# Adding the exponentials of two key tiles on GpSimd, with one set of products with ones for two tiles, in a four-layer graph network on one Trainium2 core

## The reference

```python
def _L1_gnn_ref(h, adj, Wq, bq, Wk, bk, Wv, bv, Wo, bo):
    ...
    scores = jnp.einsum('bhqd,bhkd->bhqk', q, k) * scale
    scores = jnp.where(mask, -jnp.inf, scores)
    attn = jax.nn.softmax(scores, axis=-1)
    out = jnp.einsum('bhqk,bhkd->bhqd', attn, v)
    ...
```

## Time and profile before

| | |
|---|---|
| median of 3 runs | 3092.38 us (3091.72 to 3095.64) |
| the profiled execution | 3093.04 us, its span 3091.3 us |
| TensorE busy | 2725.8 us, 88% of the span |
| VectorE busy | 2070.4 us, 67% |
| ScalarE busy | 1223.4 us, 40% |
| GpSimd busy | 824.4 us, 27% |
| mean granted TensorE clock | 0.943 |
| one step in the middle of the run | 181 us |

### The profile page before, as it was taken

How to read it: one execution, slowest core, us unless ns; L and a number is a source line. 1 busy time by engine, 2 the same in 40 slices (tenths; PEclk the granted TensorE clock), 3 DMA queues, 4 the chain that set the end, 5 groups by cost and what they waited for, 6 DMA issues and landing times.

```text
span 3091.3 us, 47649 instructions
## 1 busy us (share of the span) xinstructions
PE 2725.8 (88%) x17668; PEld 2029.7 (66%) x17668; DVE 2070.4 (67%) x5503; ACT 1223.4 (40%) x2273; POOL 824.4 (27%) x640
## 2 busy tenths in 40 slices
PE   0679989899998989989898998989899998989976
PEld 0447776767767676766767677676767767676664
DVE  3547485775848677584867758486775858677563
ACT  0224435353443535344352543435254343524341
POOL 0113231322313232232323222232322323232231
PEclk9889989999898999989899998989999898999987
DMA  4000000000000000000000000000000000000000
GB/s 124 7 14 1 8 14 1 15 8 15 8 8 14 1 15 8 15 8 8 14 1 15 8 15 8 8 14 1 14 8 15 8 8 14 1 8 8 1 8 7
DMA packets 29763, 36.74 MB, mean 12 GB/s; under 512 B 2272, under 2 KB 23648, under 8 KB 29536
## 3 DMA queue, kind: packets, MB, share of 16 engines
q1 hardware_dynamic: 29536, 33.69, 3.7%
HBM read 25.30 MB, written 8.39 MB: 11 GB/s over the span
## 4 chain that ended last, share of the span: by engine, by line
PE 57%; DVE 23%; issue 8%; ACT 6%; POOL 4%; SPq 1%; DMA 1%; DVEq 0%; POOLq 0%; ACTq 0%
PE bank L587 12%; PE bank L546 9%; PE bank L784 7%; DVE bank L1077 5%; PE bank L673 4%; PE bank L561 4%; PE bank L679 4%; PE bank L540 4%; PE bank L663 3%; PE bank L656 3%; POOL exp_b L472 3%; DVE picked L1044 2%; PE bank L793 2%; DVE o_t L1121 2%; PE bank L713 2%
## 5 line engine op out<-in xcount | busy, mean ns | idle before, releaser
L472 POOL TENSOR_TENSOR exp_b<-exp_b,edge_t 128x512 int32<-128x512 int32 x320 | 455.0, 1437 | 1075.9 <-DVE exp_b L1065 1075.9
L587 PE MATMUL bank<-vals_b,exp_b 128*128 128x257 f32 x2560 | 662.6, 404 | 75.4 <-POOL exp_b L472 67.3
L587 PEld LDWEIGHTS bank<-vals_b,exp_b 128*128 128x128 f32 x2560 | 483.4, 198 | 231.8 <-POOL exp_b L472 117.7
L923 ACT ACTIVATE h_sb<-bank,rden_g_b 128x256 f32<-128x256 f32 x320 | 151.6, 474 | 692.5 <-DVE rden_g_b L1221 692.5
L1077 DVE CUSTOM_DVE_ANT_0 bank<-bank,edge_bias 128x512 f32<-128x512 f32 x512 | 338.9, 720 | 22.4 <-PE bank L605 21.5
L1065 DVE TENSOR_TENSOR exp_b<-exp_b,low_b 128x512 f32<-128x512 f32 x320 | 271.6, 870 | 93.1 <-ACT low_b L839 90.8
L1044 DVE CUSTOM_DVE_ANT_0 picked<-bank,edge_bias 128x512 bf16<-128x512 f32 x384 | 241.5, 683 | 108.9 <-PE bank L561 108.9
L871 ACT ACTIVATE exp_a<-bank 128x512 f32<-128x512 f32 x512 | 263.9, 608 | 89.4 <-PE bank L663 89.4
L818 ACT ACTIVATE vals_b<-bank 128x512 f32<-128x512 f32 (+1 forms) x192 | 100.9, 536 | 485.5 <-PE bank L784 280.7
L460 POOL TENSOR_TENSOR rstd_a<-var_eps_a,neg_half 128x4 f32<-128x4 f32 x48 | 51.2, 1067 | 777.5 <-DVE var_eps_a L1021 777.5
L784 PE MATMUL bank<-wo_sb,ht_all 128*128 128x259 f32 x1024 | 233.6, 383 | 0.8 <-ACT ht_all L818 0.8
(11 more groups left out here) (185 smaller groups left out, 5409.5 us busy)
## 6 DMA issues: line engine op xcount, KB each, us to landing
x_t<-in_x_t SPq DMA_DIRECT2D x16, 512.0 KB, 3.6
xa<-in_x SPq DMA_DIRECT2D x16, 512.0 KB, 3.7
out<-h_sb SPq DMA_DIRECT2D x16, 512.0 KB, 2.9
exp_b<-in_adj SPq DMA_DIRECT2D x1, 1024.0 KB, 7.1
edge_t<-in_adj_t SPq DMA_DIRECT2D x1, 1024.0 KB, 9.2
wo_sb<-in_L_gnn_W_out SPq DMA_DIRECT2D x1, 1024.0 KB, 11.7
ht_all<-in_L_gnn_a_heads SPq DMA_DIRECT2D x4, 256.0 KB, 8.6
exp_a<-in_L_gnn_W_heads SPq DMA_DIRECT2D x2, 512.0 KB, 4.3
```

The source lines that it names most:

```text
L472: pool.tensor_tensor(high_exp(idx, j).bitcast(I32), high_exp(idx, j).bitcast(I32), edge_t[:, j, :], ALU.mult)\
L587: last = pe.matmul(bank(key)[:, i * width:(i + 1) * width], high_exp(idx, c)[:, t * P:(t + 1) * P], vals[:, c, 0:width], start=c == 0, sto ...
```

## The change

GpSimd adds the exponentials of key tiles 0 and 1, and of 2 and 3, head by head, into a new tile `pair_sum` (four adds of 128x512 for each of two pairs and two groups: 16 in a batch). TensorE runs its products with ones only in `pv` g 1 and `pv` g 3, on `pair_sum`. There is one `pair_sum`, so GpSimd waits for the products on the old one (`summed`, or the product of `sum`). ScalarE, before it writes over a tile of `exp_a`, waits for the products with the values and for the add that read it. `TURNS` is a new string. The tiles `first_row` and `wa`, used in the setup alone, move into `exp_b` to make room.

```diff
-TURNS = ("b2 t m3 t b2 m b m b t m b t b m3 b6 m2 a3 b m2 a m2 b2 s b2 a b a m b s b a m s a s2 a2 m s2 b s b2 s a2 m b3 m3 b2 a "
...
+TURNS = ("b2 t m3 b t b m b m b m t b3 m3 b t b m b2 m b m2 a2 b a2 m2 b3 s b a b2 m a s b a m s a s a2 m s2 b s b2 s a2 b m b2 "
...
+        pair_sum = sb("pair_sum", [P, HG, N])
...
+                for g in range(G1):
+                    for t in range(1, T, 2):
+                        for p in parts["st"]:
+                            yield "st", g, t, p
+                            for hh in heads_of("st", p):
+                                pool.wait_ge(*after(b, moved(("st", g, t, hh))))
+
+                                if t == T - 1:
+                                    pool.wait_ge(*after(b, sig.value("summed", g)))
+                                else:
+                                    for count in earlier(b, product_of(("sum", (g - 1) % G1), 0 if g else -1)):
+                                        pool.wait_ge(*count)
+                                pool.tensor_tensor(pair_sum[:, hh, :], exp1(g, t - 1, hh), exp1(g, t, hh), ALU.add)\
+                                    .then_inc(sig.raised("pair_added", (g, t // 2, hh)), 1)
...
-                    for hh in range(HG):
-                        at = slice(hh * D1, (hh + 1) * D1)
-                        last = pe.matmul(bank(("sum", g))[at, :], ones[:], exp1(g, t, hh), start=t == 0, stop=t == T - 1)
...
+                    if t % 2:
+                        for hh in range(HG):
+                            at = slice(hh * D1, (hh + 1) * D1)
+                            pe.wait_ge(*after(b, sig.value("pair_added", (g, t // 2, hh))))
+                            last = pe.matmul(bank(("sum", g))[at, :], ones[:], pair_sum[:, hh, :], start=t == 1, stop=t == T - 1)
+                        last.then_inc(filled(("sum", g)) if t == T - 1 else sig.raised("summed", g), 1)
...
+                        if old >= 0:
+                            if hh == 0:
+                                act.wait_ge(*after(b, product_of(("o", old // T)) if old % T == T - 1 else sig.value("weighed", (old // T, old % T))))
+                            act.wait_ge(*after(b, sig.value("pair_added", (old // T, old % T // 2, hh))))
```

More of the change, by code:

```diff
@@ L22 @@
 STREAMS = {"p": "pre", "m": "mid", "s": "second", "b": "back", "a": "att", "t": "tail"}
-TURNS = ("b2 t m3 t b2 m b m b t m b t b m3 b6 m2 a3 b m2 a m2 b2 s b2 a b a m b s b a m s a s2 a2 m s2 b s b2 s a2 m b3 m3 b2 a "
-         "m a m s m b2 a b m a b m a m b m a2 m a3 m a m a m a p m2 a m2 a m a m b p m2 b2 m b2 m b p m a4 m p a m a p m a2 p2 a "
-         "p a")
+TURNS = ("b2 t m3 b t b m b m b m t b3 m3 b t b m b2 m b m2 a2 b a2 m2 b3 s b a b2 m a s b a m s a s a2 m s2 b s b2 s a2 b m b2 "
+         "s b m3 b a m2 a2 b s m b2 m a b m b m a m a2 m a m a3 m a m a2 m4 a m a m b p m2 p b2 m b m b2 p m a4 m a p a m a2 p2 "
+         "m a p a p")
 AHEAD = {"pre": 2, "mid": 1, "second": 1, "back": 0, "att": 0, "tail": -1}
@@ L103, in gat_mix_program @@
         ident_r = sb("ident_r", [P, P], F32R)
-        first_row = sb("first_row", [P, P])
         first_row_r = sb("first_row_r", [P, P], F32R)
@@ L176, in gat_mix_program @@
         ah_bc = ht_all[:].rearrange("p a n -> p (a n)")[:, 0:H3 * 2 * F].rearrange("p (h j f) -> p h j f", j=2, f=F)
+        A_END = 2 * H0 + 2 * F
+        first_row = a_bc[:, A_END:A_END + P]
+        wa = a_bc[:, A_END + P:A_END + P + KF * 3 * H3].rearrange("p (k c) -> p k c", k=KF)
         adj_i = exp_b[:, SLOTS - T:SLOTS, :].bitcast(I32)
@@ L674, in weigh @@
                                          start=t == 0, stop=t == T - 1)
-                    if t == T - 1:
-                        last.then_inc(filled(("o", g)), 1)
-                    for hh in range(HG):
-                        at = slice(hh * D1, (hh + 1) * D1)
-                        last = pe.matmul(bank(("sum", g))[at, :], ones[:], exp1(g, t, hh), start=t == 0, stop=t == T - 1)
-                    if t < T - 1:
-                        last.then_inc(sig.raised("weighed", (g, t)), 1)
-                    else:
-                        last.then_inc(filled(("sum", g)), 1)
+                    last.then_inc(filled(("o", g)) if t == T - 1 else sig.raised("weighed", (g, t)), 1)
+                    if t % 2:
[4 more added lines that the diff above has]
+                        last.then_inc(filled(("sum", g)) if t == T - 1 else sig.raised("summed", g), 1)
                 yield "q", 0
@@ L866, in exps1 @@
                     for hh in heads_of("st", p):
-                        key, at = ("st", g, t, hh), g * T + t - 2
-                        for count in highest(b, product_of(key), *([] if hh else [sig.value("weighed", (at // T,
-                                             at % T)) if at >= 0 and at % T < T - 1 else product_of(("sum", at // T)) if at >= 0 else product_of("a01")])):
-                            act.wait_ge(*count)
+                        key, old = ("st", g, t, hh), g * T + t - 2
+                        act.wait_ge(*after(b, product_of(key)))
+                        if old >= 0:
+                            if hh == 0:
+                                act.wait_ge(*after(b, product_of(("o", old // T)) if old % T == T - 1 else sig.value("weighed", (old // T, old % T))))
+                            act.wait_ge(*after(b, sig.value("pair_added", (old // T, old % T // 2, hh))))
+                        elif hh == 0:
+                            act.wait_ge(*after(b, product_of("a01")))
                         act.activation(exp1(g, t, hh), bank(key)[:], ACT.Exp, scale=SCALE1).then_inc(emptied(key), 1)
@@ L1288, in program @@
     def program(order):
-        nc = _bacc.Bacc("TRN2", target_bir_lowering=False, num_devices=1, dynamic_dma_scratch_size=4096)
+        nc = _bacc.Bacc("TRN2", target_bir_lowering=False, num_devices=1, dynamic_dma_scratch_size=2048)
         arrays, args = {}, []
```

1 line of the change is left out of this document (removed).

## The result

The changed kernel takes 3255.91 us (median of 4 runs, 3246.62 to 3260.62), beside 3092.55 us for the kernel before (3091.72 to 3095.64): 1.0523 times as long, interval 1.0498 to 1.0547. It is 163 us slower. The prediction said slower by 55 us, with a range up to 3205, so the direction was right and the size was not.

A forecast was written before the change was run, and what follows sets the result against it. TensorE was taken as the bound in mid-step, waiting for others at the seam. Waits of 7.3 us less 3.9 saved lose 3.4 a batch, 55 us in 16: 3093.0 becomes 3148 us, range 3050 to 3205.

The forecast's parts named there:

- the new order (0.8 + 1.3 + 1.1): TensorE waits per batch: 0.8 us for `max_rows`, 1.3 for elu before `ht` 3 0, 1.1 for the seam's last cut.
- half the products with ones go (-3.9 + 0.5): Four TensorE product groups of 0.97 us saved per batch; 0.5 us wait at `st` 1 2, which one had covered.
- the adds and the waits for them (2.6 + 1.0): Per batch, TensorE waits 2.6 us for head 3's cut behind GpSimd's adds and 1.0 for sums at `pv` 0 3.
- The priced places: Six places in a step where TensorE would wait: 2.6, 0.5, 1.0, 0.8, 1.3 and 1.1 us, together 7.3 a batch.
- the prediction's signs: Expected in the new profile: the listed TensorE waits, among them the seam's wait for `exp_a`'s cut growing to about 2.5 us.
- The rest of `TURNS` I take at nothing: Other reordered phases cost nothing: neighbours exchanged where VectorE was waited for, its work ahead of each point unchanged.
- 3.9 us saved in a batch: Four groups of products with ones leave TensorE, 0.97 us each: 62 us in 16 batches, 2.0%.
- There, each us taken from TensorE is won: In the step's full stretch, around L1's second group, TensorE has no idle time, so time removed is gained.
- The collision, taken at nothing: VectorE and GpSimd disturbing each other: counted as 0, bounded at 3.0 us a batch for `larger` of head 2.
- the prediction's bound of 48: Worst case for the collision: three `larger` of head 2 lose 1.0 us each per batch, 48 us in all.
- Rival 2: VectorE and GpSimd collide: the priced waits plus 3.0 us a batch, 3196 us; sign `larger` mean over 1.2 us; chance 0.18.
- The clock: Waits might bring the seam's lower TensorE clock into the full stretch: not priced, only 0.10 left above the range.

The follow-up runs named there:

- e1: The kernel before with the new `TURNS` and nothing else, no adds, all products with ones: 3189.96 us, 1.031.
- e14: The kernel before in the new order, products with ones of tiles 0 and 2 left out, no adds: 3158.29 us, 1.0207.
- e13: The kernel before in its old order, products with ones of tiles 0 and 2 left out, no adds: 3080.01 us, 0.9948.
- e2: The changed kernel with the old `TURNS`, all adds kept: 3183.75 us, 1.0293 of the kernel before.
- e5: The kernel before, no adds, with only phases 0 to 64 of a step in the new order: 3148.62 us, 1.0178.
- e11: The kernel before, no adds, one move: row-maxima products of tile 2 ahead of head 0's `a3` groups: 3132.36 us, 1.0122.
- e12: The changed kernel in the old order, pairs added for the first group of heads only: 3096.54 us, 1.001 of the kernel before.
- e15: Old order, pairs in the first group only, the second group's last row maxima moved ahead of `ab` 2 1: 3078.19 us, 0.9954 of the kernel before.
- e7: The kernel before, no adds, with only phases 107 to 147 of a step in the new order: 3141.22 us, 1.0155.

## Why the prediction was right in direction and wrong in size

The four kernels before, e1, e14 and after split the 163 us into three steps, which answer to three parts of the prediction's sum:

| step | forecast, 16 batches | measured |
|---|---|---|
| the new order (0.8 + 1.3 + 1.1) | +51 | +96 |
| half the products with ones go (-3.9 + 0.5) | -54 | -32 |
| the adds and the waits for them (2.6 + 1.0) | +58 | +98 |
| sum | +55 | +162 |

The split depends on the order in which the steps are taken: the new order costs 96 us alone, 78 with half of the products with ones gone (e14 - e13) and 72 beside the adds (after - e2).

**The priced places.** They are 0.81, 0.59, 2.33, 1.24 and 2.05 us (forecast 0.8, 0.5, 2.6, 1.0 and 1.3, elu being above by the collision), and at the seam, where 1.1 was forecast, TensorE waits 1.03 and 0.98 where it waited 1.41, 0.6 more. Together they are 7.6 us in a step, and the forecast's sum was 7.3. So the missing 107 us are elsewhere. Two of the six have another cause than the one given. The 0.59 us belong to the exponential of `ab` 3 3, not to those of `st` 1 1: that size was right by luck. And at the seam the wait for the cut did not grow from 1.4 to 2.5 us, as the prediction's signs had it, but fell to 0.98, with a wait of 1.03 for a bank of `e` ahead of it.

**"The rest of `TURNS` I take at nothing" failed.** This is the largest error, 45 us. The reason given was that VectorE was the one waited for there, and its work ahead stays the same. e5 refutes it, a part with no priced place (+55), and e11 does with a single move (+39). VectorE's own order may be as good as before; TensorE, in order too, then stands before a bank that VectorE has not freed, with ready work behind.

**"3.9 us saved in a batch" failed.** "There, each us taken from TensorE is won" was read from a stretch without idle time. e13 measures 14 of the 62 us. At the traced places the products with ones had covered the release of a bank. The prediction saw this at `st` 1 2 and not at `pv` 0 0, where e12 and e13 show it.

**The collision, taken at nothing, was not nothing.** VectorE is busy 2103.8 us after and 2056.4 in e14, with the same instructions: 47 us more. That this is near the prediction's bound of 48 is chance, since the bound was worked out for `larger` alone. Here `larger` has 12 of the 47 (289.0 against 276.6), elu's first instruction 12 (115.7 against 104.2), and two small ones behind the masked maxima of L3, which the prediction did not consider, 16 and 8. First `larger` in e14, then the small instruction after, where it was 13.0 us in e14:

```profile
L1065 DVE TENSOR_TENSOR exp_b<-exp_b,low_b 128x512 f32<-128x512 f32 x320 | 276.6, 888 | 77.5 <-ACT low_b L839 77.3
```
```profile
L1068 DVE SCALAR_TENSOR_TENSOR m_max_b<-z_max_b 128x4 f32<-128x4 f32 x80 | 28.5, 356 | 2.7
```

On TensorE the waits for elu grew by 11.5 us and those for row maxima by 6.7; the rest of the 47 was not followed there. It was wrong to argue from the median: `larger` has a median of 0.69 us in both kernels, but a mean of 0.87 before, of 0.89 in e14 and of 0.93 after, so some were disturbed by the cuts all along. Rival 2 would have given 3196. Its own sign, `larger` at a mean of over 1.2 us in this stretch, did not come: for the four of head 2 it is 1.06 us, against 0.90 before.

**The clock.** The forecast left it to the range. The mean granted clock is 0.932 after against 0.943. With two levels, 1.2 and 2.4 GHz, that is 2 x 0.068 x 3254 = 442 us at the low one against 2 x 0.057 x 3091 = 352, so 90 us more, and an estimate of 45 us for the work that TensorE did at half speed. The same sum for e5 (0.933) gives 35 us, and its busy time grew by 35 with the same products. It is no fourth term: it is contained in the three. The estimate is rough, because the kernel before itself shows means from 0.939 to 0.943 at times within 4 us of each other, which is 25 us at the low level. And it does not always go with the waits: e12 and e15 have waits that the kernel before lacks, and means of 0.949 and 0.952.

**Open.** Of the 98 us for the adds, 35.5 + 11.5 + 6.7 + 26 = 80 are traced. The other 18 are not. The clock (0.934 to 0.932) could be part of them, but the difference is within what it varies from run to run. ScalarE waits 26 us for the adds before it may write over `exp_a`, and whether that reaches TensorE was not followed. Some records of one product group are missing in e14's trace, so its busy time is not used for more. Of the 48 us that e13 lacks, 37 are traced; a run with half of the products with ones and e15's exchange, which would test the largest piece, was not made. How much of e7's 48 us is norm 2 and how much the `ab0` cuts was not taken apart.
